# Two-layer transformer kernel: layer 2's q/k columns in lane-major order, and its q/k tiles loaded in 12 transfers per batch instead of 36

## The chip, the cores and the metric

The kernel runs on one core of a Trainium2 chip (trn2). The metric is the device time of one execution in microseconds (us). Smaller is better. Times shown as runs are whole executions; the profile is one further execution, read by its trace.

## The reference, cut to what matters

The input is 16 batches of 512 tokens with 128 features. Four layers follow one another, each added to its input: a linear attention, a mixture of 8 experts, a softmax attention, and a mixture of 16 experts that choose their tokens. The change is in the softmax attention, called layer 2 here (`L1_attn` in the code):

```python
q = jnp.einsum('btc,oc->bto', x, Wq).reshape(B, T, H, D)      # H = 16 heads, D = 8
k = jnp.einsum('btc,oc->bto', x, Wk).reshape(B, T, H, D)
v = jnp.einsum('btc,oc->bto', x, Wv).reshape(B, T, H, D)
att = jnp.einsum('bqhd,bkhd->bhqk', q, k) * SCALE
att = jnp.where(band_mask, -inf, att)
att = softmax(att, axis=-1)
out = jnp.einsum('bhqk,bkhd->bqhd', att, v)
```

## The kernel before, in words

**Stages.** The work of the first three layers is pipelined over the batches. `looped` runs, for each batch, an x phase and a y phase on every engine; 13 of the passes are a hardware loop (`Fori(1, BATCH - 2)`, line L277), the first and last ones are written out. In one pass the x phase holds the expert layer of batch i+1 (L669, L677, L685, L695 on TensorE), the row maxima of the attention of batch i, and the end of batch i-1. The y phase holds the attention scores and outputs of batch i, the linear attention of batch i+2, and the q, k, v of batch i+1. After the loop come the choice of tokens (L1420 to L1561) and the 16 experts, which the change doesn't touch. Each engine has its own instruction list, written out by hand; they meet at semaphores only.

**q and k in three parts.** Layer 2's q and k are computed as 128 features x 512 tokens in `facc` (`r_q` L706, `r_k` L710, with `w_q1` and `w_k1`). ScalarE, VectorE and GpSimd split them into three bf16 parts each, whose sum is the fp32 value, in `qkp` (L1029, L1368, L486, L488). SyncE stores `qkp` to `qk_parts` in HBM, q and k apart (`part_dmas`, L313), waits for both, and loads it back in another layout (`back_dmas`, L317 to L331).

**QT and KT.** These two tiles hold, for each head and token, 72 rows: all 9 pairs of a q part i and a k part j, with 8 lanes each. The scores of a head are then one matmul over 72 (or 75) rows. In `back_dmas` a feature of `qk_parts` is (head, lane), the lane being the inner index; a transfer takes part i of q, or part j of k, to 8 partitions, one per lane, and 8 heads of 512 tokens in each:

```python
for i in range(PARTS):
    for j in range(PARTS):
        r = (i * PARTS + j) * HD
        for t, w, part in ((QT, 0, i), (KT, 1, j)):
            sp.dma_start(t[r:r + HD, heads], qk_parts[b, w, part].rearrange("(h d) t -> d h t", d=HD)[:, heads])
```

So half 0 (heads 0 to 7) and half 1 (heads 8 to 15) take 18 transfers each. Half 0 may start when the scores of the first 20 fills of the y phase are done, half 1 when all 40 are (`s_st`, last written by L582).

**Who waits for them.** The x phase on TensorE begins with `fill(0)`: scores L585 (with the mask L587) into one of three banks `ba`, from fill 0 on with half 0 and from fill 20 on with half 1. VectorE reduces each bank to row maxima (L1263 to L1268), and TensorE may write a bank again only then. SyncE's own order in a pass is: `load_x` (xin, L359), `residual_dmas` (L352), `max_dmas` (QT from nmT, L339), `row_dmas` (L345), `part_dmas` (L313), `back_dmas` half 0, half 1 (L330). VectorE needs xin at L1135 in the x phase.

Of the kernel before, what the change touches and what calls it, by code (L numbers as in the profile page):

```python
# [14 lines left out]
F32, BF16, F16, I32, I16 = mybir.dt.float32, mybir.dt.bfloat16, mybir.dt.float16, mybir.dt.int32, mybir.dt.int16  # L15
# [4 lines left out]
P = 128  # L20
BATCH, SEQ, D = 16, 512, 128
# [3 lines left out]
HEADS, HD = 16, 8  # L25
# [10 lines left out]
PARTS = 3  # L36
# [8 lines left out]
def build_kernel(nc, a, out):  # L45
    ctx = ExitStack()
    with ctx:
# [5 lines left out]
        def sb1(name, shape, dt=F32):  # L53

            return early.enter_context(nc.sbuf_tensor(name, shape, dt))
# [2 lines left out]
            return ctx.enter_context(nc.semaphore(name))  # L58


        qk_parts = nc.dram_tensor("qk_parts", (BATCH, 2, PARTS, P, SEQ), BF16, kind="Internal").ap()
        xn_rows = nc.dram_tensor("xn_rows", (TOK, ROW), F32, kind="Internal").ap()
        out_rows = out.rearrange("b s d -> (b s) d")
        lists = nc.dram_tensor("lists", (E1, CAP), I32, kind="Internal").ap()
# [3 lines left out]
        facc = ctx.enter_context(nc.psum_tensor("facc", [P, 512], F32))  # L68
# [33 lines left out]
        w_q1 = sb1("w_q1", [P, D])  # L102
        w_k1 = sb1("w_k1", [P, D])
        w_v1 = sb1("w_v1", [P, D])
        w_o1 = sb1("w_o1", [P, D])
        router_w = sb1("router_w", [P, E1])
        router_b = sb1("router_b", [P, E1])
# [41 lines left out]
        b_nT = sb1("b_nT", [P, SEQ])  # L149
        qkp = sb1("qkp", [P, 2, PARTS, SEQ], BF16)  # L150
        qkr = sb1("qkr", [P, 2, SEQ])
        vp = sb1("vp", [P, Q, HEADS, 32])
        QT = sb1("QT", [P, HEADS, SEQ], BF16)
        KT = sb1("KT", [P, HEADS, SEQ], BF16)
# [31 lines left out]
        def sb3(name, shape, dt=F32):  # L186
# [54 lines left out]
        names = """s_wfront s_wexperts s_wback s_cst s_one s_scal s_x s_lnf s_xres s_varf s_rsf s_T1 s_nT1 s_kvq s_kvqe s_sq  # L241
            s_kqn s_kvt s_kvm s_qT s_qnT s_kvo s_kvoc s_at0 s_x1 s_x1n s_T2 s_nT2 s_lgm s_lge s_exf s_lgx s_gp s_gTp s_gT
            s_h1 s_h3 s_gb s_gbc s_sil s_t s_h s_hs s_ym s_yT s_yTt s_x2 s_fc
            s_pad s_lnb s_varb s_rsb s_T3 s_nT3 s_q s_k s_v s_p1 s_r1 s_p2 s_p3 s_vp s_qkw s_qk0 s_qk1 s_S s_red s_nmp s_nmt
            s_nmT s_mx0 s_mx1 s_st s_exp s_pv s_oT s_tr s_norm s_aTt s_aT s_wo s_x3 s_row s_T4 s_nT4 s_l1 s_l1c
            s_g1x s_g1e s_rowd s_mstep s_x3d s_gn s_gnd
            s_vart s_rst s_rstep s_tc s_rden s_LTt s_cnt s_tot s_sr s_gtc s_gtt s_eqt s_rc s_slT s_slot s_ramp s_hot s_hot_t s_list s_keys s_cand s_cnt3 s_set s_gth s_gthc s_low s_diag s_gatec s_gj s_found s_idx s_bc1 s_ldw s_ldr
# [1 line left out]
        S = {n: sem(n) for n in names}  # L249
# [40 lines left out]
        def _(sp):  # L290
# [17 lines left out]
            def part_dmas(b):  # L308

                for w in range(2):  # L310
                    sp.wait_ge(S["s_p3"], 2 * b + w + 1)
                    apart(sp)
                    sp.dma_start(qk_parts[b, w].rearrange("c p t -> p c t"), qkp[:, w]).then_inc(S["s_qkw"], 16)  # L313
                sp.wait_ge(S["s_qkw"], 32 * b + 32)
                apart(sp)

            def back_dmas(b, half):  # L317

                if isinstance(b, int) and b == 0:
                    sp.wait_ge(S["s_pad"], 3)  # L320
                else:

                    sp.wait_ge(S["s_st"], FILLS * b - (1 - half) * FILLS // 2)
                    apart(sp)
                heads = slice(half * HEADS // 2, (half + 1) * HEADS // 2)
                for i in range(PARTS):
                    for j in range(PARTS):
                        r = (i * PARTS + j) * HD
                        for t, w, part in ((QT, 0, i), (KT, 1, j)):
                            sp.dma_start(t[r:r + HD, heads], qk_parts[b, w, part].rearrange("(h d) t -> d h t", d=HD)[:, heads])\  # L330
                              .then_inc(S[f"s_qk{half}"], 16)  # L331

            def max_dmas(b, half):

# [267 lines left out]
        def _(pe):  # L602
# [95 lines left out]
            def r_turn(r):  # L698
                if isinstance(r, int) and r == 0:
                    pe.wait_ge(S["s_wback"], BW)  # L700
                pe.wait_ge(S["s_lnb"], r + 1)
                transposes(facc, b_n, "s_T3")

            def r_q(r):
                pe.wait_ge(S["s_nT3"], r + 1)
                pe.matmul(facc[:], lhsT=w_q1[:], rhs=b_nT[:], start=True, stop=True).then_inc(S["s_q"], 1)  # L706

            def r_k(r):
                pe.wait_ge(S["s_r1"], 2 * r + 1)
                pe.matmul(facc[:], lhsT=w_k1[:], rhs=b_nT[:], start=True, stop=True).then_inc(S["s_k"], 1)  # L710

            def r_v(r):
                pe.wait_ge(S["s_r1"], 2 * r + 2)
# [41 lines left out]
            def x_phase(f, b, t, g):  # L755
                def fill(n):
                    if b is None:
                        return
                    if n == 0:
                        pe.wait_ge(S["s_qk0"], 16 * 2 * PARTS * PARTS * (b + 1))  # L760
                        pe.wait_ge(S["s_exp"], FILLS * b)
                    if n == FILLS // 2:
                        pe.wait_ge(S["s_qk1"], 16 * 2 * PARTS * PARTS * (b + 1))
                    if n >= 3:
                        pe.wait_ge(S["s_red"], FILLS * b + n - 2)
                    scores(pe, b, n, False)
# [201 lines left out]
        def _(act):  # L968
# [37 lines left out]
            def y_phase(b, f, r, t):  # L1006
# [18 lines left out]
                                   ACT.Square).then_inc(S["s_sq"], 1)  # L1025
                exps(1)
                if r is not None:
                    act.wait_ge(S["s_qkw"], 32 * r)
                    copy(qkp[:, 0, 0], facc[:], "s_q", r + 1, "s_p1")  # L1029
                exps(2)  # L1030
                if r is not None:
# [59 lines left out]
        def _(dve):  # L1091
# [261 lines left out]
            def r_norm(r):  # L1353
                rc.start(r)
                if isinstance(r, int) and r == 0:
                    dve.wait_ge(S["s_wback"], BW)
                dve.wait_ge(S["s_x2"], r + 1)
                apart(dve)
                stats(rc, x3_of(r), b_st, b_mv)
                dve.tensor_scalar(b_ve[:], b_mv[:, :, 1], EPS, None, ALU.add).then_inc(S["s_varb"], 1)  # L1360
# [270 lines left out]
```

## Time and profile before

| what | value |
|---|---|
| median of 3 runs | 2110.64 us (2103.11 to 2110.79) |
| the profiled execution's own time | 2108.77 us |
| its span, first to last instruction | 2107.0 us |
| mean granted TensorE clock | 0.883 of 2.4 GHz |
| TensorE, VectorE, ScalarE, GpSimd busy | 77%, 59%, 37%, 24% of the span |
| DMA: bytes, packets | 86.56 MB, 113452 |
| HBM read, written | 58.95 MB, 25.72 MB |

In the profile PE is TensorE's matmuls and PEld its weight loads, DVE is VectorE, ACT ScalarE, POOL GpSimd and SP SyncE; a q behind a name (SPq, DVEq) is that engine's sequencer, which issues DMAs and branches. Busy time says how much an engine did, the waits and the chain of waits say what it stood for. "Issue" is time in which an engine waited for nothing that the profile records. Stretches are in microseconds from the start of the span.

### The profile page before, as it was taken

How to read it: one execution, taken by the hardware profiler on the slowest of the kernel's cores; microseconds unless marked ns; L12 is line 12 of the kernel's file. 1: busy time of each engine (PE TensorE's matmuls, PEld its weight loads, DVE VectorE, ACT ScalarE, POOL GpSimd, SP SyncE). 2: the span in 40 equal slices, each digit the busy share in tenths (PEclk: the TensorE clock that was granted, in tenths of full speed). 3: DMA queues.
4: the chain of work that ended last, by engine and by line, in shares of the span. 5: the costliest groups of instructions: out<-in, count | busy, mean ns of one | idle time of the engine just before them, and what ended most of it. 6: DMA issues, size and time to landing. Idle time of an engine off the chain costs nothing.

```text
span 2107.0 us, 34513 instructions
## 1 busy us (share of the span) xinstructions
PE 1619.2 (77%) x10136; PEld 907.4 (43%) x10136; DVE 1236.6 (59%) x3717; ACT 778.5 (37%) x1387; POOL 501.6 (24%) x487
## 2 busy tenths in 40 slices
PE   3869898979787878888888888798889781137765
PEld 2335454535353434444444444444454441135554
DVE  5456767666667575757575757575766526861111
ACT  1225252525252525252525252525254242134331
POOL 2311212121212121212121212121212002006887
PEclk7879999989899989899989899999999875568897
DMA  2041321313131313130313130404031400024444
GB/s 63 16 50 33 40 50 27 50 26 51 25 52 25 52 24 57 19 59 18 58 18 59 17 61 15 64 12 63 13 58 20 65 7 10 0 39 86 89 89 59
DMA packets 113452, 86.56 MB, mean 41 GB/s; under 512 B 21569, under 2 KB 107841, under 8 KB 113345
## 3 DMA queue, kind: packets, MB, share of 16 engines
q1 hardware_dynamic: 102080, 76.58, 21.4%
q0 software_dynamic: 11264, 8.92, 3.2%
q14 instruction: 86, 0.70, 0.2%
q8 instruction: 22, 0.36, 0.1%
HBM read 58.95 MB, written 25.72 MB: 40 GB/s over the span
## 4 chain that ended last, share of the span: by engine, by line
PE 47%; DVE 17%; issue 17%; POOL 5%; DMA 4%; ACT 4%; SPq 2%; DVEq 1%; ACTq 0%; POOLq 0%
PE ba L580 6%; PE bo L839 5%; PE facc L695 5%; PE fa L669 5%; PE ba L585 5%; PE fa L685 5%; POOL out L552 3%; SPq L330 2%; ACT probs L1015 2%; DVE passed L1460 2%; DVE nm L1263 2%; PE ba L587 2%; PE ba L582 2%; POOL got L522 2%; DMA KT<-qk_parts 1%
## 5 line engine op out<-in xcount | busy, mean ns | idle before, releaser
L585 PE MATMUL ba<-KT,QT 72*128 72x512 bf16 (+3 forms) x1024 | 262.2, 320 | 182.5 <-DVE nm L1263 129.2
L1015 ACT ACTIVATE probs<-ba 128x512 f32<-128x512 f32 x640 | 330.5, 640 | 97.7 <-PE ba L582 96.9
L459 POOL TENSOR_TENSOR hh<-th,gb 128x512 f32<-128x512 f32 x128 | 161.9, 1265 | 697.5 <-ACT gb L971 427.0
L580 PE MATMUL ba<-QT,KT 75*128 75x512 bf16 (+3 forms) x1024 | 253.3, 310 | 35.2 <-ACT probs L1015 28.7
L1263 DVE TENSOR_REDUCE nm<-ba 128x1 f32<-128x512 f32 x256 | 174.6, 682 | 179.5 <-issue 131.2
L585 PEld LDWEIGHTS ba<-KT,QT 72*128 72x128 bf16 x1024 | 105.0, 103 | 344.5 <-DVE nm L1263 155.8
L587 PE MATMUL ba<-mask_q,identb 128*128 128x128 bf16 x1024 | 200.8, 230 | 0.0
L987 ACT ACTIVATE sil<-fa 128x512 f32<-128x512 f32 x160 | 95.4, 596 | 274.9 <-PE fa L669 274.8
L582 PE MATMUL ba<-mask_k,identb 128*128 128x128 bf16 x1024 | 195.5, 224 | 0.0
L669 PE MATMUL fa<-f_nT,w 128*128 128x512 f32 x320 | 187.1, 669 | 1.2 <-ACT sc L1046 1.2
L685 PE MATMUL fa<-f_nT,w 128*128 128x512 f32 x320 | 181.1, 649 | 0.0
L971 ACT ACTIVATE gb<-fa 128x512 f32<-128x512 f32 x128 | 76.5, 598 | 278.7 <-PE fa L677 245.4
L580 PEld LDWEIGHTS ba<-QT,KT 75*128 75x128 bf16 x1024 | 101.7, 99 | 156.5 <-ACT probs L1015 104.7
L695 PE MATMUL facc<-hh,w 128*128 128x512 f32 x320 | 166.2, 602 | 0.0
L839 PE MATMUL bo<-probs,vp 128*32 128x512 f32 (+3 forms) x2048 | 155.2, 444 | 0.8 <-DVE ao L1384 0.8
L1265 DVE TENSOR_REDUCE nm<-ba 128x1 f32<-128x384 f32 x256 | 140.6, 549 | 25.1 <-PE ba L587 25.0
L587 PEld LDWEIGHTS ba<-mask_q,identb 128*128 128x128 bf16 x1024 | 106.3, 104 | 81.7 <-issue 79.5
L452 POOL TENSOR_TENSOR b_rs<-b_ve,mhalf 128x4 f32<-128x4 f32 x48 | 48.5, 1010 | 336.4 <-DVE b_ve L1360 229.1
L1375 DVE COPY oT<-bo 128x512 f32<-128x512 f32 x64 | 44.1, 690 | 116.4 <-PE bo L839 115.4
L552 POOL DMA_INDIRECT out<-contrib,cur x64 | 100.7, 1573 | 30.5 <-issue 18.6
L839 PEld LDWEIGHTS bo<-probs,vp 128*32 128x32 f32 x2048 | 60.8, 111 | 99.2 <-issue 69.9
L582 PEld LDWEIGHTS ba<-mask_k,identb 128*128 128x128 bf16 x1024 | 102.6, 100 | 1.6 <-issue 0.7
(284 smaller groups left out, 2643.2 us busy)
## 6 DMA issues: line engine op xcount, KB each, us to landing
QT<-qk_parts SPq DMA_DIRECT2D x288, 64.0 KB
KT<-qk_parts SPq DMA_DIRECT2D x288, 64.0 KB
qk_parts<-qkp SPq DMA_DIRECT2D x32, 384.0 KB, 2.5
fc<-in_L_ffn_fc_weight SPq DMA_DIRECT2D x32, 256.0 KB
xin<-in_L_attn_x SPq DMA_DIRECT2D x16, 256.0 KB, 13.4
out<-x SPq DMA_DIRECT2D x16, 256.0 KB, 2.3
xn_rows<-row SPq DMA_DIRECT2D x16, 256.0 KB, 2.4
w<-in_L_w SPq DMA_DIRECT2D x3, 640.0 KB, 6.7
```

The source lines that it names most:

```text
L459: pool.tensor_tensor(hh[:, e % 2], th[:, e % 2], gb[:, e % 2], ALU.mult).then_inc(S["s_h"], 1)
L552: pool.indirect_dma_start(out_rows, bass.IndirectOffsetOnAxis(cur[k][:, c:c + 1], 0), contrib[k % 2][:, c], None, compute_op=ALU.add).then ...
L580: pe.matmul(bank[:, col:col + w], lhsT=KT[0:K_ROWS, head, blk * P:(blk + 1) * P], rhs=QT[0:K_ROWS, head, blk * P:], start=True, stop=False)
L582: last = pe.matmul(bank[:, col:col + P], lhsT=identb[:], rhs=mask_k[:], start=False, stop=True)
L585: pe.matmul(bank[:, col:col + w], lhsT=QT[0:QK_ROWS, head, blk * P:(blk + 1) * P], rhs=KT[0:QK_ROWS, head, 0:w], start=True, stop=False)
L587: last = pe.matmul(bank[:, col + w - P:col + w], lhsT=identb[:], rhs=mask_q[:], start=False, stop=True)
L669: pe.matmul(fa[0][:], lhsT=w1[:, e], rhs=f_nT[:], start=True, stop=True).then_inc(S["s_h1"], 1)
L685: pe.matmul(fa[1][:], lhsT=w3[:, e], rhs=f_nT[:], start=True, stop=True).then_inc(S["s_h3"], 1)
L695: pe.matmul(facc[:], lhsT=w2[:, e], rhs=hh[:, e % 2], start=e == 0, stop=e == U0 - 1).then_inc(S["s_ym"], 1)
L839: last = pe.matmul(bo[32 * j:32 * j + 32, blk * P:], lhsT=vp[:, blk, 4 * k + j], rhs=prob_block(4 * k + j, blk), start=blk == 0, stop=blk ...
L1015: act.activation(probs[:, pair % 3, f_], ba[n % 3][:], ACT.Exp, scale=SCALE).then_inc(S["s_exp"], 1)
L1263: last = dve.tensor_reduce(nm[:, 3, h:h + 1], bank[:], X, ALU.max, negate=True)
```

## The change

Layer 2's q and k features are ordered (lane, head) instead of (head, lane). A new tile `w_qk` holds both weights with their columns reordered; VectorE makes it once, by two copies in front of batch 0's `r_norm`, and TensorE waits for them once. `qk_parts` has five places per batch for q and for k. All three parts of each are stored to the first three, and a third store puts k's parts 0 and 1 into places 3 and 4. The 9 pairs are now (part p of q, part (shift + p) mod 3 of k), so that each of three shifts takes three neighbouring places at once: 24 partitions of QT or KT, with 8 heads x 512 tokens that lie together in HBM (8 KB). Half 0 and half 1 take 6 transfers each. SyncE's wait before the loads counts three stores.

```diff
-        qk_parts = nc.dram_tensor("qk_parts", (BATCH, 2, PARTS, P, SEQ), BF16, kind="Internal").ap()
+        qk_parts = nc.dram_tensor("qk_parts", (BATCH, 2, 2 * PARTS - 1, P, SEQ), BF16, kind="Internal").ap()
...
+        w_qk = sb1("w_qk", [P, 2, HD, HEADS])
...
                 for w in range(2):
                     sp.wait_ge(S["s_p3"], 2 * b + w + 1)
                     apart(sp)
-                    sp.dma_start(qk_parts[b, w].rearrange("c p t -> p c t"), qkp[:, w]).then_inc(S["s_qkw"], 16)
-                sp.wait_ge(S["s_qkw"], 32 * b + 32)
+                    sp.dma_start(qk_parts[b, w].rearrange("c p t -> p c t")[:, 0:PARTS], qkp[:, w]).then_inc(S["s_qkw"], 16)
+                sp.dma_start(qk_parts[b, 1].rearrange("c p t -> p c t")[:, PARTS:], qkp[:, 1, 0:PARTS - 1]).then_inc(S["s_qkw"], 16)
+                sp.wait_ge(S["s_qkw"], 48 * b + 48)
                 apart(sp)
...
-                for i in range(PARTS):
-                    for j in range(PARTS):
-                        r = (i * PARTS + j) * HD
-                        for t, w, part in ((QT, 0, i), (KT, 1, j)):
-                            sp.dma_start(t[r:r + HD, heads], qk_parts[b, w, part].rearrange("(h d) t -> d h t", d=HD)[:, heads])\
-                              .then_inc(S[f"s_qk{half}"], 16)
+                for shift in range(PARTS):
+                    r = slice(shift * PARTS * HD, (shift + 1) * PARTS * HD)
+                    for t, w, part in ((QT, 0, 0), (KT, 1, shift)):
+                        rows = qk_parts[b, w, part:part + PARTS].rearrange("c (d h) t -> (c d) h t", h=HEADS)
+                        sp.dma_start(t[r, heads], rows[:, heads]).then_inc(S[f"s_qk{half}"], 16)
...
                 if isinstance(r, int) and r == 0:
                     pe.wait_ge(S["s_wback"], BW)
+                    pe.wait_ge(S["s_wqk"], 2)
...
-                pe.matmul(facc[:], lhsT=w_q1[:], rhs=b_nT[:], start=True, stop=True).then_inc(S["s_q"], 1)
+                pe.matmul(facc[:], lhsT=w_qk[:, 0].rearrange("p d h -> p (d h)"), rhs=b_nT[:], start=True, stop=True).then_inc(S["s_q"], 1)
...
-                pe.matmul(facc[:], lhsT=w_k1[:], rhs=b_nT[:], start=True, stop=True).then_inc(S["s_k"], 1)
+                pe.matmul(facc[:], lhsT=w_qk[:, 1].rearrange("p d h -> p (d h)"), rhs=b_nT[:], start=True, stop=True).then_inc(S["s_k"], 1)
...
-                        pe.wait_ge(S["s_qk0"], 16 * 2 * PARTS * PARTS * (b + 1))
+                        pe.wait_ge(S["s_qk0"], 16 * 2 * PARTS * (b + 1))
...
-                        pe.wait_ge(S["s_qk1"], 16 * 2 * PARTS * PARTS * (b + 1))
+                        pe.wait_ge(S["s_qk1"], 16 * 2 * PARTS * (b + 1))
...
-                    act.wait_ge(S["s_qkw"], 32 * r)
+                    act.wait_ge(S["s_qkw"], 48 * r)
...
                 if isinstance(r, int) and r == 0:
                     dve.wait_ge(S["s_wback"], BW)
+                    for w, t in enumerate((w_q1, w_k1)):
+                        dve.tensor_copy(w_qk[:, w], t[:].rearrange("p (h d) -> p d h", d=HD)).then_inc(S["s_wqk"], 1)
```

SyncE, in the loop body: the end of the stores and the start of half 0, before. ISA stands for register and semaphore work, and a DMA's shape is partitions x elements.

```order
L313 DMA qk_parts<-qkp 128x3x512
L314 ISA
L323 ISA [waits s_qkw]
L330 DMA QT<-qk_parts 8x8x512 [waits s_st]
L330 DMA KT<-qk_parts 8x8x512
L330 DMA QT<-qk_parts 8x8x512
```

The same place now:

```order
L314 DMA qk_parts<-qkp 128x3x512
L315 ISA
L315 DMA qk_parts<-qkp 128x2x512
L316 ISA
L325 ISA [waits s_qkw]
L332 DMA QT<-qk_parts 24x4096 [waits s_st]
L332 DMA KT<-qk_parts 24x4096
L332 DMA QT<-qk_parts 24x4096
```

A third store stands ahead of the wait for the stores, and each load is 24 x 4096 elements in one run where it was 8 x 8 x 512; the loop body has 12 of them where it had 36.

VectorE, at the written-out start of batch 0's part in layer 2, now (x<-facc is the residual sum that the expert layer ends with):

```order
L1353 TENSOR_TENSOR x<-facc,x 128x512 [waits s_yTt]
L1360 COPY w_qk<-w_q 128x128 [waits s_wback]
L1360 COPY w_qk<-w_k 128x128
L1137 BN_STATS b_st<-x 128x6 [waits s_x2]
```

The two copies stand between the residual sum and the statistics; before, the statistics followed at once, and they took the wait for the weights (`s_wback`) with them.

## Rows read from the trace of the kernel before

**Rows 1.** The page: busy us of each engine (share of the span) and instructions

```profile
PE 1619.2 (77%) x10136; PEld 907.4 (43%) x10136; DVE 1236.6 (59%) x3717; ACT 778.5 (37%) x1387; POOL 501.6 (24%) x487
```

**Rows 2.** The table of waits: engine, line <- releaser: us in total, times, longest

```profile
DVE nm L1263 <- issue: 131.2, 12, 12.4
PE ba L585 <- DVE nm L1263: 129.2, 17, 11.8
```

**Rows 3.** The chain of waits, 1020 to 1065 us: start, us, what

```profile
1047.39 0.06 DVEq L277
1047.45 11.83 issue
```

**Rows 4.** Loop line L277, 1040 to 1065, then VectorE's, whole span: ns min/median/max, starts

```profile
L277 PEldq COMPARE_BRANCH  x1: 207/207/207, 1044.4 to 1044.4; - x1
L277 PEldq FUSED_REGOPS  x1: 50/50/50, 1044.7 to 1044.7; - x1
...
L277 DVEq COMPARE_BRANCH  x13: 55/63/63, 319.5 to 1572.0; - x13
```

**Rows 5.** The timeline of SyncE's queue, 1024 to 1050 us: start, us, what

```profile
1024.63 0.32 SPq L330 DMA_DIRECT2D QT<-qk_parts  x1
...
1039.24 0.28 SPq L330 DMA_DIRECT2D QT<-qk_parts  x1
...
1049.50 0.40 SPq L359 DMA_DIRECT2D xin<-in_L_attn_x  x1
```

**Rows 6.** Stretches of one pass: us, busy us of each engine, PEclk, DMA share, GB/s

```profile
1036.00:1047.40 11.40, 8.18 (x76) 5.12 (x74) 7.10 (x36) 3.87 (x8) 0.00 (x0) 1.00 0.59 64
1047.40:1059.30 11.90, 2.02 (x13) 0.93 (x11) 0.20 (x1) 2.36 (x3) 0.00 (x0) 0.67 0.65 80
1059.30:1065.00 5.70, 4.86 (x14) 2.41 (x15) 4.33 (x9) 1.08 (x2) 0.94 (x1) 0.50 0.31 47
```

**Rows 7.** DMA issues: count, KB each, median us to landing

```profile
QT<-qk_parts SPq DMA_DIRECT2D x288, 64.0 KB
...
qk_parts<-qkp SPq DMA_DIRECT2D x32, 384.0 KB, 2.5
...
xin<-in_L_attn_x SPq DMA_DIRECT2D x16, 256.0 KB, 13.4
out<-x SPq DMA_DIRECT2D x16, 256.0 KB, 2.3
```

**Rows 8.** Stretches of other transfers: the first weights, and a store of qk_parts

```profile
11.00:14.00 3.00, 0.00 (x0) 0.00 (x0) 2.42 (x11) 0.21 (x1) 0.51 (x1) 1.00 1.02 418
1022.00:1024.00 2.00, 2.00 (x20) 1.68 (x18) 0.29 (x1) 1.36 (x3) 0.00 (x0) 1.00 0.58 197
```

**Rows 9.** First pass of the loop, its branch stall (chain), and half 0's first load

```profile
220.50:319.50 99.00, 89.19 (x572) 47.21 (x571) 68.38 (x210) 42.16 (x77) 19.90 (x18) 0.97 0.28 46
...
295.18 0.33 SPq L330 DMA_DIRECT2D QT<-qk_parts  x1
...
319.60 7.66 issue
```

**Rows 10.** First pass: xin's wait, TensorE behind it, the clock; and a 128x128 operation

```profile
236.60 0.87 DVE L1135 BATCH_NORM_STATS2 f_st<-xin 128x6 f32<-128x128 f32 x4 [5.25 <-DMA xin<-in_L_attn_x]
...
238.98 0.39 PE L585 MATMUL ba<-KT,QT 72*128 72x256 bf16 x1 [4.20 <-DVE nm L1266]
...
236.00:242.00 6.00, 3.02 (x9) 1.32 (x10) 5.19 (x18) 0.00 (x0) 1.48 (x2) 0.75 0.00 0
...
1039.77 0.29 DVE L1384 TENSOR_TENSOR ao<-bo,rden 128x128 f32<-128x128 f32 x1
```

**Rows 11.** Batch 0 and the last batch: TensorE's waits for KT

```profile
125.45 0.61 PE L585 MATMUL ba<-KT,QT 72*128 72x512 bf16 x1 [10.73 <-DMA KT<-qk_parts]
...
1661.03 0.61 PE L585 MATMUL ba<-KT,QT 72*128 72x512 bf16 x1 [4.88 <-DMA KT<-qk_parts]
...
1678.62 0.61 PE L585 MATMUL ba<-KT,QT 72*128 72x512 bf16 x1 [4.29 <-DMA KT<-qk_parts]
```

More of the change, by code:

```diff
@@ L243, in build_kernel @@
             s_h1 s_h3 s_gb s_gbc s_sil s_t s_h s_hs s_ym s_yT s_yTt s_x2 s_fc
-            s_pad s_lnb s_varb s_rsb s_T3 s_nT3 s_q s_k s_v s_p1 s_r1 s_p2 s_p3 s_vp s_qkw s_qk0 s_qk1 s_S s_red s_nmp s_nmt
+            s_pad s_wqk s_lnb s_varb s_rsb s_T3 s_nT3 s_q s_k s_v s_p1 s_r1 s_p2 s_p3 s_vp s_qkw s_qk0 s_qk1 s_S s_red s_nmp s_nmt
             s_nmT s_mx0 s_mx1 s_st s_exp s_pv s_oT s_tr s_norm s_aTt s_aT s_wo s_x3 s_row s_T4 s_nT4 s_l1 s_l1c
```

## The prediction

> **What bounds the kernel now.** I read the page first [rows 1]: TensorE is busy 77% of the span and VectorE 59%, so neither fills it. The table of waits comes next [rows 2]. Among VectorE's waits one is released by nothing that the profile shows: "issue", 131.2 us in 12 times, always before the first maxima reduction (L1263). TensorE's longest wait, 129.2 us in 17 times, is on that same reduction. The chain of waits [rows 3] gives the place: VectorE's branch at the end of the loop body (DVEq L277) at 1047.39, then 11.83 us of nothing, then the first instruction of the next pass. The records of the loop's own line [rows 4] show that TensorE has no such stall: its branch is at 1044.4 and its counter for the next pass at 1044.7. VectorE branches 13 times, 319.5 to 1572.0 us, so a pass is 104.4 us; 12 branches are taken, 12 stalls follow, 10.9 us each.
>
> Why so long? SyncE's queue [rows 5] shows the load of QT and KT: half 0 is issued from 1024.63, half 1 from 1039.24, and xin only behind it at 1049.50. Meanwhile the DMA traffic is flat at 64 GB/s [rows 6]. Both halves are 36 transfers of 64 KB [rows 7], 2.36 MB, 37 us at 64 GB/s: from 1024.6 to about 1062. A store of 128 partitions of the same 1 KB runs reaches 197 GB/s, and the weights at the start 418 GB/s [rows 8], so the loads' shape is slow, not the memory. What is issued behind them is late too: xin, 256 KB, lands after 13.4 us at the median, an equal store after 2.3 [rows 7]. The stall fits: VectorE resumes 34.8 us after the first load of half 0 in this pass. In the first stalled pass half 0 is issued at 295.18, 24.3 us ahead of the branch where it is 22.8 here, and the stall there is 7.66 us, ending 32 us after the first load [rows 9]. So the end of the stall follows the backlog of the loads, not the branch. I read it as VectorE fetching the loop's first instructions through DMA engines that are choked by the loads. The Trainium skill ("Runtime: NRT & Kernel Launch", Instruction fetch mechanics) says that a taken branch out of a small window forces such a fetch; the trace agrees, in that the stall follows the taken branch on VectorE.
>
> **The change part by part.**
>
> *Loads.* Per batch 36 transfers of 8 partitions x 8 runs of 1 KB become 12 of 24 partitions, one 8 KB run each; bytes stay 2.36 MB. Their rate is not in the trace, so I bound it. From below: 64 GB/s as now, 18.4 us a half. From above: the 418 GB/s of the weights, 2.8 us. Between them I scale 64 GB/s by the partitions written at once, 8 to 24: a factor of 3, 192 GB/s, 6.1 us a half. I take this, since it is nearest to the store at 197 GB/s in the same pass [rows 8]. If half of the factor comes, 1.5, it is 96 GB/s and 12.3 us: the slow case. A factor of 1.5 is also what a rule of the skill gives ("DMA: Bandwidth & Descriptors", Why a DMA increments its semaphore by 16 and not by 1): the engines used are the largest number up to 16 that divides the outer size, 8 for 8 and 12 for 24. The skill's "SBUF — State Buffer" (Door 1) instead counts ports, four neighbouring partitions to one: 2 before, 6 now, a factor of 3. By the first rule alone the time would be that of the slow case below, 2037 us, by the second that of the forecast.
>
> *SyncE.* 36 issues become 12. Half 1 still starts at 1039.24, when TensorE's last use of the tiles frees it, and with 6 issues in place of 18 is out some 2 us later instead of 10; xin goes out there, not at 1049.5.
>
> *The third store* (256 KB, issued behind the second, before the loads): 0.4 us to issue and 1.3 us at 197 GB/s, 1.6 us later for half 0. In the loop this is covered: half 0 would land at 1024.6 + 1.6 + 6.1 + 2 = 1034.3, and TensorE branches into the next pass at 1044.4 [rows 4]. Without that cover it costs 1.6 us, as in batch 0.
>
> *The two reordering copies* on VectorE happen once; a 128x128 piece takes 0.29 us [rows 10]: 0.6 us. The matmuls keep their shape (L706, L710), so 0.
>
> *The branch stall.* Half 1 has left the queues by 1039.2 + 6.1 = 1045.3, ahead of VectorE's branch at 1047.4. What is left is the fetch itself. Below it is bounded by TensorE's 0.3 us [rows 4], above by the backlog at 96 GB/s: half 1 ends at 1051.5, 4.1 us after the branch, plus the fetch, 6.6. For an unhindered fetch I take 2.5 us, what a store of qk_parts needs to land [rows 7]. The stall falls from 10.9 to 2.5: 8.4 us a pass.
>
> *The clock behind it.* In the stall TensorE's granted clock falls to 0.50 (1.2 GHz) for the 5.7 us after it [rows 6]: 4.9 us busy at half speed, 2.4 us lost. TensorE's gap becomes some 2.5 us in place of about 11. In the first pass it idled 4.20 us, and the six microseconds around show 0.75, half of them at full clock [rows 10]; with a gap shorter than that I count the clock as kept. The bound below is 0.
>
> *A check on the sum.* The first pass in the loop has no branch before it, and is 99.0 us long [rows 9]. In it VectorE waits 5.25 us for xin, itself behind the loads, and the clock is at half for half of 6 us, 3.0 of it, and 1.5 lost [rows 10]. Without both: 92.2 us. A pass with the 2.5 us fetch is then 94.7, against 104.4: 9.7 us. The terms above give 10.8; I take 9.7, since it is a whole pass as it ran. What is late next inside the pass is again TensorE with the maxima, as now.
>
> *Outside the stalls.* First pass: 5.25 + 1.5 = 6.8. Batch 0: TensorE waits 10.73 us for KT [rows 11]; half 0 took 1.18 MB / 64 GB/s = 18.4 us and takes 6.1 + 1.6 for the third store: 10.7 less, of which I count 10 (by the slow bound 18.4 - 13.9 = 4.5). Last batch: two waits for KT, 4.88 and 4.29: 9.2 us.
>
> **Sum:** 12 x 9.7 + 6.8 + 10 + 9.2 - 0.6 = 142 us off the profiled execution's 2108.8 (span 2107.0), 1967 us. The median of the runs is 2110.6, 0.1% more; a difference of 0.5% (10.5 us) is about what a measurement here can tell from none.
>
> **The rivals.**
>
> *The loads gain only half.* 12.3 us a half: the stall is 6.6, the clock falls as before. 12 x 4.3 + 6.8 + 4.5 + 9.2 = 72 us: 2037. For it: the store at 197 GB/s works on all 128 partitions, the loads on 24. Against it: the same loads on 8 have 64 already. Chance 0.14.
>
> *The fetch has a price of its own.* Some 11 us per taken branch whatever the queues hold; the gain is 6.8 + 10 + 9.2 = 26 us: 2083. For it: the mean of 10.9 and the longest of 12.4 us [rows 2] lie close together, as a constant would. Against it: the one of 7.66 us, and xin, late by the same amount. The skill's rule stands on this rival's side ("DMA: Bandwidth & Descriptors", Queues, rings and completion order): an engine takes turns between its rows packet by packet, so a fetch should not stand behind a whole backlog. Chance 0.10.
>
> *The loads are the same.* The transfer may be cut up again below the program, and end at 64 GB/s; then only issues are saved, and the time stays within a few us of 2109. Against it: SyncE's list has one 24 x 4096 transfer in place of three. Chance 0.04.
>
> *Slower: long runs into few partitions move at less than before.* Backlog ends at half 0's issue plus 2.36 MB over the rate, and half 0 is now 1.6 us later, so it decides below 2.36 MB / 35.4 us = 67 GB/s. At 50 GB/s it ends at 1073.4 instead of 1062: 12 more per pass, 12 x 12 + 12 in the first pass + some 10 in the first and last batch: 2275. For it: an 8 KB run goes into one partition, and no row has such a run. Against it: the weights' runs, 5 KB to a partition, at 418 GB/s [rows 8]. Chance 0.04.
>
> **How the numbers follow.** Forecast: 0.68, 1967 us, its own range 1925 (a fetch of 0.3 us: 2.2 less in 12 passes, and the 1.1 between the two sums, 40 us) to 1990 (a fetch of 4.5 us: 24 more). The slow-load case reaches 2037, so I close the range at 1925 to 2042; outside are the three rivals at 2083 and above, together 0.18. Faster by over 0.5%: 0.68 + 0.14 + 0.10 = 0.92; within: 0.04; slower: 0.04.
>
> **What would show each step.** VectorE's "issue" wait before L1263 near 30 us in 12 times, not 131; behind its branch the loop counter 2 to 4 us later; the slices behind the issue of a half near 190 GB/s and empty after 6 us; xin landing in 3 to 5 us; the granted clock near 1.00 through the start of a pass; TensorE's waits for KT gone; a pass of 94 to 95 us. Wrong would be: the loads short and the stall still near 11 (the third case), or slices behind the issue under 100 GB/s (the second).

## The result and the profile after

| | kernel before | changed kernel |
|---|---|---|
| median of 4 runs each, one chip | 2106.88 us (2095.60 to 2110.79) | 1978.94 us (1976.47 to 1981.08) |
| ratio, 95% interval | | 0.9401, 0.9359 to 0.9442 |
| the profiled execution | 2108.77 us, span 2107.0 | 1980.44 us, span 1978.7 |
| mean granted TensorE clock | 0.883 | 0.907 |

The change takes 6.0% off. 1967 us was forecast, within 1925 to 2042: the time is 12 us above the point and inside the range. One run in this document, e2's of 2054.1 us, lies over 1.5% above the fastest of its kernel (2022.8 us); e2's median and ratio leave it out.

The page of the changed kernel, its busy times, against [rows 1]:

```profile
PE 1604.5 (81%) x10090; PEld 903.9 (46%) x10136; DVE 1237.3 (63%) x3719; ACT 778.6 (39%) x1387; POOL 501.7 (25%) x487
```

VectorE does what it did, in a span that is 128.3 us shorter: what went was waiting, not work. TensorE's busy time is down by 15 us; how much of that is the clock and how much the 46 matmul records fewer (10090 for 10136, some 7 us at their mean of 0.16 us) is not told apart here. The tables of waits, against [rows 2]:

```profile
DVE nm L1265 <- issue: 38.3, 12, 3.7
...
PE ba L586 <- DVE nm L1265: 43.5, 22, 3.9
```

The stalls are still 12, one for each taken branch, but 38.3 us together and not 131.2. TensorE's wait on the same reduction went with them, from 129.2 to 43.5. The chain of waits, 865 to 885 us, against [rows 3], and the loop line (now L278) over the whole span, against [rows 4]:

```profile
872.38 0.06 DVEq L278
872.45 3.44 issue
875.88 0.06 DVEq L278
...
876.00 0.70 DVE nm L1265
```

```profile
L278 DVEq COMPARE_BRANCH  x13: 55/63/63, 296.6 to 1452.5; - x13
```

A pass is (1452.5 - 296.6) / 12 = 96.3 us, where it was 104.4. The twelve stalls of the chain lie between 2.83 and 3.75 us, 3.2 in the mean. SyncE's queue over 820 to 880 us, against [rows 5]:

```profile
841.59 5.65 SPq L314 DMA_DIRECT2D qk_parts<-qkp  x2
847.42 0.37 SPq L315 DMA_DIRECT2D qk_parts<-qkp  x1
850.41 0.36 SPq L332 DMA_DIRECT2D QT<-qk_parts  x1
...
852.68 0.30 SPq L332 DMA_DIRECT2D KT<-qk_parts  x1
864.21 0.30 SPq L332 DMA_DIRECT2D QT<-qk_parts  x1
...
866.48 0.30 SPq L332 DMA_DIRECT2D KT<-qk_parts  x1
867.37 0.40 SPq L360 DMA_DIRECT2D xin<-in_L_attn_x  x1
```

Each half is out in 2.6 us, and xin is issued 5.0 us ahead of VectorE's branch at 872.38 instead of 2.1 behind it. What the engines move meanwhile (columns as in [rows 6]):

```profile
850.40:856.50 6.10, 6.06 (x66) 3.70 (x58) 2.08 (x6) 3.40 (x9) 0.00 (x0) 1.00 0.65 146
864.20:870.40 6.20, 5.38 (x58) 3.58 (x56) 5.12 (x25) 1.52 (x4) 0.00 (x0) 1.00 0.73 153
870.40:872.40 2.00, 2.00 (x9) 0.79 (x9) 1.84 (x12) 1.04 (x1) 0.00 (x0) 1.00 0.71 148
872.40:876.00 3.60, 0.71 (x7) 0.26 (x5) 0.19 (x2) 1.32 (x3) 0.00 (x0) 0.98 0.31 57
876.00:880.00 4.00, 3.04 (x9) 1.53 (x11) 3.21 (x7) 0.16 (x1) 0.00 (x0) 0.50 0.01 2
```

150 GB/s where 64 stood before, 8 us a half, and then xin: the traffic still reaches a little past the branch (57 GB/s over the stall). The last row is what the forecast did not count: TensorE's granted clock is still at 0.50 (1.2 GHz) behind the stall. The landings, against [rows 7]:

```profile
QT<-qk_parts SPq DMA_DIRECT2D x96, 192.0 KB
...
xin<-in_L_attn_x SPq DMA_DIRECT2D x16, 256.0 KB, 7.1
qk_parts<-qkp SPq DMA_DIRECT2D x16, 256.0 KB, 2.7
```

xin lands after 7.1 us, before 13.4. No wait for xin or for KT stands in the tables any more; those of [rows 10] and [rows 11] are gone. The first pass of the loop, without a branch ahead of it, and the two behind it, against [rows 9]:

```profile
205.40:296.60 91.20, 85.46 (x569) 45.86 (x571) 68.42 (x210) 41.88 (x77) 19.91 (x18) 1.00 0.19 46
296.60:391.20 94.60, 85.38 (x569) 45.88 (x571) 68.49 (x210) 41.80 (x77) 19.89 (x18) 1.00 0.19 45
391.20:488.90 97.70, 87.85 (x569) 46.83 (x570) 68.54 (x210) 41.74 (x77) 19.89 (x18) 0.97 0.18 44
```

**Where the 128 us come from.** Branches and spans cut the two profiles into the same pieces:

| piece | before | after | gain | forecast |
|---|---|---|---|---|
| start to the loop | 220.5 | 205.4 | 15.1 | 10 - 0.6 |
| first pass | 99.0 | 91.2 | 7.8 | 6.8 |
| 12 passes with a stall | 1252.5 | 1155.9 | 96.6 | 116.4 |
| last branch to the end | 535.0 | 526.2 | 8.8 | 9.2 |
| span | 2107.0 | 1978.7 | 128.3 | 141.8 |

So all of the shortfall lies in the twelve passes, 8.1 us each and not 9.7, and 5.7 us came back ahead of the loop.

**The fetch itself is in the profile.** The prediction called the stall "released by nothing that the profile shows". The view of the DMA queues does show it: beside SyncE's queue there is one of the kind "instruction", with packets of 8 KB. Narrow windows around the stalls find exactly one such packet inside each: in all 12 of before, all 12 of the changed kernel, the same in the runs e4 to e8 told below, and in the nine stalls of e3 that the chain of waits shows. One pass of each (us):

| kernel | branch | the packet moves | VectorE goes on |
|---|---|---|---|
| before | 1047.4 | 1056.7 | 1059.3 |
| e6 (8 partitions, 8 KB runs) | 914.0 | 921.0 | 923.0 |
| changed kernel | 872.4 | 873.9 | 875.9 |
| e7 (queues nearly empty) | 870.2 | 871.2 | 873.0 |

With nearly empty queues the packet moves about 1 us after the branch and VectorE goes on 1.8 us later. Over all stalls the second part stays between 1.7 and 2.9 us; it is the first part that grows, to between 7.7 and 9.9 us in eleven stalls of before (5.4 in its first). And it grows by what is queued ahead: in before the packet moves when SyncE's queue has moved 2.16 to 2.30 MB of the 2.29 to 2.36 MB that it had been given by the time of the branch (2.59 of 2.62 in the first stall, where xin was issued ahead of the branch). It does not wait for the 0.32 to 0.46 MB that are then left in eleven of the stalls, xin, issued behind the branch, among them: in the pass shown they move until about 1062.5, 3 us after VectorE went on.

### The profile page after: what moved, and what is told of

The parts are those of the page before. It is cut to its first block, busy times and chain, and to the rows that moved or that the text cites. A ratio compares the mean times of both kernels' runs of the same rounds, so it can differ in the third digit from the quotient of the medians.

```text
span 1978.7 us, 33763 instructions
## 1 busy us (share of the span) xinstructions
PE 1604.5 (81%) x10090; PEld 903.9 (46%) x10136; DVE 1237.3 (63%) x3719; ACT 778.6 (39%) x1387; POOL 501.7 (25%) x487
## 4 chain that ended last, share of the span: by engine, by line
PE 50%; DVE 19%; issue 12%; POOL 5%; ACT 4%; DMA 2%; DVEq 1%; SPq 0%; ACTq 0%; POOLq 0%
PE ba L581 6%; PE bo L841 6%; PE ba L586 5%; PE facc L696 5%; PE fa L686 5%; PE fa L670 5%; POOL out L553 3%; ACT probs L1017 2%; DVE nm L1265 2%; PE ba L583 2%; DVE passed L1464 2%; PE ba L588 2%; POOL got L523 2%; PE ba L957 1%; PE bo L848 1%
## 5 line engine op out<-in xcount | busy, mean ns | idle before, releaser
L1017 ACT ACTIVATE probs<-ba 128x512 f32<-128x512 f32 x640 | 330.3, 636 | 97.3 <-PE ba L583 96.5
L586 PE MATMUL ba<-KT,QT 72*128 72x512 bf16 (+3 forms) x1024 | 256.3, 313 | 68.2 <-DVE nm L1265 43.5
L1265 DVE TENSOR_REDUCE nm<-ba 128x1 f32<-128x512 f32 x256 | 174.8, 683 | 70.0 <-issue 38.3
L588 PE MATMUL ba<-mask_q,identb 128*128 128x128 bf16 x1024 | 196.8, 226 | 0.0
L670 PE MATMUL fa<-f_nT,w 128*128 128x512 f32 x320 | 183.8, 658 | 1.2 <-ACT sc L1048 1.2
L686 PE MATMUL fa<-f_nT,w 128*128 128x512 f32 x320 | 177.5, 637 | 0.1
L1572 DVE TENSOR_TENSOR ysum<-ba,fb 128x512 f32<-128x512 f32 x16 | 11.1, 692 | 158.5 <-PE ba L957 158.5
```

The source lines that it names most:

```text
L586: pe.matmul(bank[:, col:col + w], lhsT=QT[0:QK_ROWS, head, blk * P:(blk + 1) * P], rhs=KT[0:QK_ROWS, head, 0:w], start=True, stop=False)
L588: last = pe.matmul(bank[:, col + w - P:col + w], lhsT=identb[:], rhs=mask_q[:], start=False, stop=True)
L670: pe.matmul(fa[0][:], lhsT=w1[:, e], rhs=f_nT[:], start=True, stop=True).then_inc(S["s_h1"], 1)
L686: pe.matmul(fa[1][:], lhsT=w3[:, e], rhs=f_nT[:], start=True, stop=True).then_inc(S["s_h3"], 1)
L1017: act.activation(probs[:, pair % 3, f_], ba[n % 3][:], ACT.Exp, scale=SCALE).then_inc(S["s_exp"], 1)
L1265: last = dve.tensor_reduce(nm[:, 3, h:h + 1], bank[:], X, ALU.max, negate=True)
```

## The experiments

Theory A is that of the forecast: a taken branch makes VectorE fetch the loop's first instructions, the fetch waits behind the loads of QT and KT, and so the stall ends when the loads issued ahead of the branch are through. Rivals: the stall belongs to the work at the top of the pass; the gain comes from the loads' own waits; run length or the number of transfers matters, not the partitions. All nine were run on the changed kernel unless "before" is said.

| run | edit | us | ratio to before, 95% | stalls, mean us | pass |
|---|---|---|---|---|---|
| before | | 2106.9 | | 10.9 | 104.4 |
| changed kernel | | 1978.9 | 0.940 (0.936 to 0.944) | 3.2 | 96.3 |
| e1 | VectorE's loop written out | 1919.1 | 0.907 (0.903 to 0.912) | none | 91.1 |
| e2 | before, VectorE's loop written out | 2028.4, three runs | 0.960 (0.953 to 0.967) | none | |
| e3 | before, no loads of half 1 | 1984.9, one run | | 2.8 | 95.2 |
| e5 | no loads of half 1 | 1970.1, one run | | 2.7 | 95.7 |
| e4 | 24 partitions, 1 KB runs | 1998.2 | 0.943 (0.939 to 0.947) | 3.9 | 97.7 |
| e6 | 8 partitions, 8 KB runs | 2062.8 | 0.977 (0.973 to 0.981) | 8.9 | 102.5 |
| e8 | no third store | 1980.0 | 0.937 (0.934 to 0.940) | 3.2 | 96.6 |
| e9 | TensorE kept busy at the branch | 1970.4 | 0.930 (0.926 to 0.934) | 2.7 | 95.6 |
| e7 | xin issued earlier | 1970.2 | 0.930 (0.927 to 0.933) | 2.7 | 95.5 |

The ratios are against runs of before on the same chip (medians 2115.2 for e1 to e4, 2115.8 for e5, e6, e8 and e9, 2116.6 for e7). The last two columns are of the profiled execution; a pass is the distance of VectorE's first to last branch, divided by 12 (for e1 that of SyncE's stores of `row`). On the chip of the first comparison before took 2106.9 us, on these 9 us more. So a difference of up to some 9 us between 1978.9 and a whole time of this table can be the chip's, and by the ratios it can come out otherwise; the stalls and passes of the profiles are the firmer measure there.

**e1 and e2: no branch on VectorE.** The other engines keep their loops.

```diff
+            if unrolled:
+                for i in range(1, BATCH - 2):
+                    x_phase(i + 1, i, i - 1, i + 2)
+                    y_phase(i, i + 2, i + 1, i - 1)
...
-            looped(dve, x_phase, y_phase)
+            looped(dve, x_phase, y_phase, unrolled=True)
```

> The changed kernel with VectorE's list alone written out for all 13 passes, so that it takes no branch. Theory A (the stall at the start of a pass is an instruction fetch that a taken branch forces): VectorE's issue wait before the first maxima, 38.3 us in 12 times, goes to under 3 us, a pass takes 91 us as the first one does (205.4 to 296.6) in place of 96.3, and the time falls by about 60 us to 1919. Rival B (the stall belongs to the start of the x phase, whatever the branch): the wait stays near 3.2 us in each pass, 1979. Rival C (a list of some 8000 instructions that is streamed once falls behind): the issue waits spread over other lines, 1960 or more.

> The kernel before with the same edit and its 36 short loads. Theory A: the 131.2 us of issue wait are gone although the backlog is as long as before; every pass is then like the first, 99.0 us instead of 104.4, since VectorE still waits some 5 us for xin behind the loads: about 2044. If xin is late in the first pass only, 1962. Rival B: stall and time stay, 2107. Rival C (a backlog of 37 us also delays the fetches of a straight list, past what is fetched ahead): issue waits of several us at other lines of VectorE, 2070 or more.

e1 hit its number. SyncE's stores of `row`, once a batch, show the pass, in the changed kernel first and then in e1:

```profile
831.41 0.43 SPq L346 DMA_DIRECT2D xn_rows<-row  x1
928.94 0.41 SPq L346 DMA_DIRECT2D xn_rows<-row  x1
1025.48 0.41 SPq L346 DMA_DIRECT2D xn_rows<-row  x1
```

```profile
898.27 0.41 SPq L351 DMA_DIRECT2D xn_rows<-row  x1
988.77 0.41 SPq L351 DMA_DIRECT2D xn_rows<-row  x1
```

97.5 and 96.5 us become 90.5; over the loop e1's lie between 90.5 and 92.4. 12 x (96.3 - 91.2) = 61 us were to be had, and 1978.9 - 1919.1 = 60 came (69 by the ratios). The stall is the branch's, and so is the loss of clock behind it. e1 beats both kernels. e2 separates the two costs of the slow loads in before. Its branch stalls are gone too, and what is left are waits on the loads themselves:

```profile
DVE f_st L1140 <- DMA xin<-in_L_attn_x: 77.0, 14, 8.3
```

```profile
PE ba L590 <- DMA KT<-qk_parts: 33.0, 14, 10.5
```

77 us for xin (landing after 16.0 us at the median, 13.4 in before) are nearly all new: before has 8.4 us in two waits, for in the loop the stall covered them. TensorE's wait for KT was 26.4 us in 13 times and is 33.0 in 14. So slow loads cost time without the fetch as well. 2028.4 us lie 16 us below the 2044 of theory A, and far from those of its rivals. Of the 196 us between before (2115.2) and e1, writing out the loop alone gives 85 (71 to 99, by the interval of the ratio), the loads alone 128; so some 17 us are in both. (The profile is of the run of 2054.1 us, so only its waits are read.)

**e3 and e5: less behind the branch.** Both leave out the loads of half 1 after batch 0; TensorE's wait for half 1 then asks for batch 0's only.

```diff
+                if half == 1 and not (isinstance(b, int) and b == 0):
+                    return
```

> The kernel before without the loads of half 1 after batch 0: heads 8 to 15 of later batches are computed with batch 0's q and k. SyncE's waits stay, the branch stays. Theory A with the backlog: half 0's 1.18 MB at 64 GB/s are through by 1043, before VectorE's branch at 1047.4, so the stall falls from 10.9 to about 3 us, as in the changed kernel, and the time to some 1980 to 2000. Rival (the price of the fetch depends on the kernel's shape of transfers or on the number of issues, not on what is queued at the branch): the stall stays over 8 us and the time over 2060.

> The changed kernel without the loads of half 1 after batch 0 (heads 8 to 15 of later batches use batch 0's q and k). In the changed kernel half 1 is issued 8.2 us before VectorE's branch and needs about 8 us at 150 GB/s. Theory (a part of the 3.2 us stall is still the end of that backlog; the kernel before with half 1 left out had 2.7): the stall falls to 2.7, the time by 6 to 12 us. Rival (3.2 us is the fetch alone): stall and time stay within 0.1 and 3 us.

In before, with the loads of half 0 still 8 partitions wide, the stall falls from 10.9 to between 2.69 and 3.05 us (e3, the nine stalls that its tables put to "issue"), although nothing in front of the branch or behind it changed on VectorE. That rules out a fixed price near 11 us. It takes away 18 issues as well as their bytes; that the bytes count is read from the packets above and from e6. In the changed kernel the same edit takes off only 0.5 us of stall (3.2 to 2.7) and 0.6 a pass, 12 x 0.6 = 7 us; the one run is 9 us shorter. The two ends meet at 2.7 us, the fetch with the queues empty. The rows of waits, of e3 and of e5:

```profile
DVE nm L1265 <- issue: 24.8, 9, 3.0
```

```profile
DVE nm L1267 <- issue: 32.6, 12, 3.0
```

**e4 and e6: which part of the new shape counts.** The change makes two things at once: 24 partitions for 8, and 8 KB runs for 1 KB. e4 keeps the first (heads of the two halves lie alternately in HBM, so that a half's runs are 1 KB), e6 the second (each load is cut into three of 8 partitions).

```diff
-                        rows = qk_parts[b, w, part:part + PARTS].rearrange("c (d h) t -> (c d) h t", h=HEADS)
-                        sp.dma_start(t[r, heads], rows[:, heads])
+                        rows = qk_parts[b, w, part:part + PARTS].rearrange("c (d h x) t -> (c d) h x t", h=HEADS // 2, x=2)
+                        sp.dma_start(t[r, heads], rows[:, :, half])
```

```diff
+                        for p in range(PARTS):
+                            r = (shift * PARTS + p) * HD
+                            rows = qk_parts[b, w, part + p].rearrange("(d h) t -> d h t", h=HEADS)
+                            sp.dma_start(t[r:r + HD, heads], rows[:, heads])
```

> The changed kernel with runs of 1 KB: the halves' heads are interleaved in the column order, so each of the 12 transfers still goes to 24 partitions, but reads 8 runs of 1 KB for each. Theory (the rate follows the partitions a transfer spreads over): the slices behind an issue stay near 150 GB/s as in the changed kernel (146 and 153), the stall stays at 3.2 to 4 us, 1979 to 1985. Rival (the length of the runs made the loads fast): the rate falls to 64 to 96 GB/s, the stall to 6 us or more, 2030 to 2100.

> The changed kernel with each load cut into three of 8 partitions: 8 KB runs as now, 36 transfers per batch as before. Theory (the rate follows the partitions a transfer spreads over): 60 to 75 GB/s behind an issue, a stall of 9 to 12 us, and a time near the kernel before, 2080 to 2110. Rival (the long runs matter): over 100 GB/s and a stall under 6 us, 2030 or less.

Stretches behind the issue of half 0 and of half 1, first of e4, then of e6:

```profile
863.90:869.50 5.60, 5.60 (x64) 3.54 (x62) 1.20 (x4) 2.90 (x8) 0.00 (x0) 1.00 0.50 117
878.20:884.00 5.80, 4.99 (x56) 3.29 (x54) 4.73 (x23) 1.51 (x4) 0.00 (x0) 1.00 0.53 122
```

```profile
892.00:899.00 7.00, 6.91 (x71) 4.02 (x64) 2.85 (x10) 4.30 (x11) 0.00 (x0) 1.00 0.45 83
...
905.80:914.00 8.20, 7.39 (x65) 4.36 (x64) 6.92 (x35) 2.53 (x5) 0.00 (x0) 1.00 0.50 88
914.00:920.00 6.00, 0.78 (x7) 0.31 (x5) 0.23 (x1) 1.39 (x3) 0.00 (x0) 0.91 0.61 106
```

| | 1 KB runs | 8 KB runs |
|---|---|---|
| 8 partitions | 64 GB/s (before) | 83 to 88 GB/s (e6) |
| 24 partitions | 117 to 122 GB/s (e4) | 146 to 153 GB/s (changed) |

The partitions give a factor of 1.7 to 1.9 in either column, the run length one of 1.25 to 1.4 in either row, together 2.3 to 2.4. The DMA engines' mean busy share is 0.59 in before ([rows 6]), 0.45 to 0.50 in e6, 0.50 to 0.53 in e4 and 0.65 to 0.73 in the changed kernel; what it is in the number of partitions that makes the rate, no run tells apart. By e6 8 KB runs alone would have given 53 us, by e4 24 partitions alone 117 us. Both outcomes lie outside what was expected of them: e4 was put at no more than 1985 and is 1998, e6 at no less than 2080 and is 2063. Run length weighs more than theory A had it. In e4 part of it is the issue, for each of its transfers has 192 runs of 1 KB where the changed kernel's has 24 of 8 KB:

```profile
881.89 0.78 SPq L332 DMA_DIRECT2D QT<-qk_parts  x1
882.86 0.78 SPq L332 DMA_DIRECT2D KT<-qk_parts  x1
```

0.78 us for each and not 0.30 (before's transfers, of 64 runs, took 0.28): a half takes 5.5 us to issue instead of 2.6. At 120 GB/s it needs 9.8 us to move, so the issue is not all of it.

The backlog rule holds in e6. The chain of waits, 905 to 930 us:

```profile
914.02 0.06 DVEq L278
914.09 8.87 issue
```

Half 0 was issued at 892.03. 2.36 MB at 85 GB/s are 27.8 us, to 919.8; the fetch's packet moves at 921.0 and the stall ends at 923.0. xin (issued at 914.35, behind the branch) is in the queues too. The changed kernel's stall has 3.2 us with loads that end about at the branch, e4's 3.9 with loads that end a little later, e6's 8.9 and before's 10.9 with loads that end well behind it: the same order throughout.

**e8: the third store.** KT takes its parts from the same three places for every shift.

```diff
-                sp.dma_start(qk_parts[b, 1].rearrange("c p t -> p c t")[:, PARTS:], qkp[:, 1, 0:PARTS - 1]).then_inc(S["s_qkw"], 16)
-                sp.wait_ge(S["s_qkw"], 48 * b + 48)
+                sp.wait_ge(S["s_qkw"], 32 * b + 32)
...
-                    for t, w, part in ((QT, 0, 0), (KT, 1, shift)):
+                    for t, w, part in ((QT, 0, 0), (KT, 1, 0)):
```

> The changed kernel without the third store; KT's loads take places 0 to 2 for every shift, so that k's parts are paired wrongly and six of the nine products stand twice or not at all. Theory (the third store is covered everywhere but in batch 0): half 0 is issued 1 to 1.6 us sooner, TensorE does not notice, time equal to the changed kernel's within 4 us. Rival (256 KB more to HBM per batch hold up what follows them): 10 us less or more.

1980.01 against 1978.94 us, stalls of 3.2 us in both, a pass of 96.6 against 96.3: 4.2 MB of stores more cost nothing that can be told from the chips' difference. In the pass at 844 us half 0 is issued 8.1 us after the stores begin, where the changed kernel takes 8.8: 0.8 us sooner and not 1 to 1.6.

**e9: the clock.** In the loop's passes TensorE does 14 matmuls into a bank that nobody reads, as soon as VectorE's last work ahead of the branch is done.

```diff
+                if t is not None and not isinstance(t, int):
+                    pe.wait_ge(S["s_norm"], 4 * t + 4)
+                    for _ in range(14):
+                        pe.matmul(bo[:], lhsT=identb[:], rhs=pick[:, 0:4].rearrange("p e c -> p (e c)"), start=True, stop=True)
```

> The changed kernel with 14 matmuls of 128x512 bf16 on TensorE in each pass of the loop, some 3 us at full clock, between the gates' transposes and fill 3, into a bank that is overwritten before it is read: work that nobody needs, in the gap that VectorE's stall leaves. Theory (the 1.9 us per pass beyond stall and straight pass are TensorE at half clock after its gap): the granted clock stays at 1.00 over the start of a pass, a pass takes 94.4 to 95.0 us in place of 96.3, 1957 to 1965. Rival (those 1.9 us are something else, the clock costs nothing here): 1977 or more.

The clock at the top of the pass is kept, as meant. What that is worth stays unclear: by the medians 8.6 us come of it, of the 14 to 22 expected, by the ratios 21, and e9's four runs lie between 1958.5 and 1977.4 us. The profile is of the longest of them. Stretches of it from one pass: ahead of the branch, and across the stall.

```profile
865.00:874.00 9.00, 8.18 (x58) 4.48 (x59) 6.48 (x33) 1.73 (x4) 0.00 (x0) 0.81 0.79 160
874.00:878.00 4.00, 3.84 (x21) 1.76 (x21) 1.29 (x4) 1.56 (x3) 0.00 (x0) 1.00 0.02 5
```

In this run the loss has moved. Ahead of the branch, where the changed kernel has 1.00, the clock now stands at 0.81 over 9 us: 1.7 us lost there, in place of 1.9 behind the branch. 91.2 + 2.7 + 1.7 = 95.6, which is the pass of e9. The kernel before has the same once, ahead of its first branch and without any filler: 0.83 over the 9.8 us from 309.8 to 319.6. Why the clock falls there, with TensorE busy for 8.2 of 9 us, no run here tells. The gain that is left in this run is the shorter stall (2.7 for 3.2): the queues are empty by then (5 GB/s in the second row).

**e7: xin ahead of the stores.** One question was left: does xin, issued just before the branch, hold up the fetch? (SyncE's last pass is written out for it.)

```diff
-            with sp.Fori(1, BATCH - 2) as i:
-                load_x(i + 2)
+            load_x(3)
+
+            def one_pass(i, last=False):
...
+                if not last:
+                    load_x(i + 3)
                 part_dmas(i + 1)
```

> The changed kernel, with SyncE issuing xin one batch earlier and ahead of the stores of qk_parts in its pass, so that nothing but the loads of half 1 stands in the DMA queues at VectorE's branch; nothing is left out. Theory (the 3.2 us stall is a fetch of 2.7 us plus about 0.5 us behind the end of the loads and xin): xin's 256 KB no longer share the engines with the fetch, the stall falls by at most 0.5 us, the issue wait in front of the maxima stays between 32 and 39 us in 12 times, the clock at a pass's start stays near 0.8, and the time is 1970 to 1981 us. Rival (xin, issued at the branch, is what lengthens the fetch and the rest of the fetch is small): the stall falls to 1.5 us or less and the clock is kept: 1940 us or less.

1970.2 us is the lower end of what theory A said, and 12 x (96.3 - 95.5) = 10 us come from the passes of the profiles, so this gain is not the chip's. xin lands in 2.9 us, and the stall is at its floor. The chain of waits, 868 to 876 us, and the stretches across and behind the stall:

```profile
870.18 0.06 DVEq L278
870.25 2.70 issue
```

```profile
870.20:873.00 2.80, 0.71 (x7) 0.27 (x5) 0.19 (x1) 1.32 (x3) 0.00 (x0) 1.00 0.02 3
873.00:876.00 3.00, 2.19 (x6) 1.03 (x7) 2.94 (x7) 0.00 (x0) 0.00 (x0) 0.65 0.01 3
876.00:880.00 4.00, 3.78 (x18) 2.07 (x18) 2.32 (x7) 1.68 (x3) 1.26 (x1) 0.84 0.00 0
```

3 GB/s during the stall, and it still takes 2.70 us: that is the fetch with nothing ahead of it. The clock behind it gives away 3.0 x 0.35 + 4.0 x 0.16 = 1.7 us even so. Of the edits tried, only taking the branch away removed both (e1).

## Why the prediction was right, and which steps left it 12 us low

**What bounds the kernel: right.** The stall at VectorE's taken branch was the bound, and its length was the loads issued ahead of it: the fetch's packet moves when they are through, e3 empties the queues behind half 0 and the stall falls to its floor without any change to the loads' shape, and e1 takes the branch away and the whole cost goes. Where the prediction has the whole backlog, up to 1062, as what the stall ends with, it is only the part ahead of the branch: the packet moves at 1056.7. "The fetch has a price of its own" (0.10) falls as a price of 11 us; as a price of 2.7 it is true. The 2.5 that the forecast took was borrowed from the landing of a store, a transfer of another kind, so that it lies this near is in part luck. The Trainium skill ("Runtime: NRT & Kernel Launch", Instruction fetch mechanics) says that a taken branch to a target outside a small window forces a fetch. The trace agrees: each stall holds one packet of the instruction queue, and without the branch (e1) there is no stall. The Trainium skill's rule that a DMA engine takes turns between its rows packet by packet ("DMA: Bandwidth & Descriptors", Queues, rings and completion order) would, as the prediction read it, have the fetch pass the backlog. The trace differs: the fetch's packet, in a queue of its own, moves 9.2 us after the branch, with 2.18 of the 2.29 MB ahead of it through. (That xin is late behind the loads says nothing on this rule, since both are in SyncE's queue.)

**Loads, a factor of 3 and 192 GB/s: the size was off.** They reach 146 to 153 GB/s, a factor of 2.3 to 2.4, and a half takes 8 us. It lies between the two factors that the forecast weighed, 1.5 and 3. By e4 and e6 neither describes it: partitions give 1.7 to 1.9 of it and run length, for which the forecast had counted nothing, 1.25 to 1.4. For the time this mattered little: half 1 now ends at the branch instead of 2 us ahead of it. That the miss cost so little is in part luck: at half the factor the forecast itself had a stall of 6.6 us.

**The branch stall, 10.9 to 2.5: off by 0.7.** Measured 3.2: 2.7 of fetch (e5, e7, e9) and 0.5 because the last of the loads and xin, issued ahead of the branch, are still moving. 12 x 0.7 = 8 us.

**The clock "counted as kept": wrong, and the largest miss.** TensorE waits up to 3.9 us for the first reduction now, and in eleven of the twelve passes the clock falls behind it, after the shortest stall (2.83 us) too; only the first pass with a stall, of 3.32 us, keeps it (94.6 us, where the next takes 97.7). The pass of 96.3 less 91.2 and 3.2 leaves 1.9 us, 12 x 1.9 = 23 us. The forecast leaned on one row, the 4.20 us of [rows 10] with half of the following six microseconds at full clock, and read "half kept" as "kept when the gap is shorter". The stalls of 2.7 us in e7 (clock 0.65 behind the one shown) show that it is not. The passes without a stall were 1 us shorter than the forecast had them (91.2 against 92.2): the first pass of before had also lost 1.7 us of clock ahead of its branch (0.83 over 9.8 us), which the forecast's 1.5 did not hold. So the "whole pass as it ran" of 94.7 took the miss back in part, by chance: 0.7 + 1.9 - 1.0 = 1.6 a pass, which is the 20 us of the table within rounding.

**Outside the stalls: 6 us better.** TensorE's waits for KT are gone as said. Ahead of the loop 15.1 us came where 9.4 stood: TensorE's waits for KT were 10.9 us and all went, and the forecast had overlooked a wait for xin in batch 0. The chain of waits of before, 120 to 221 us, shows it once it is asked for:

```profile
128.30 14.73 DMA xin<-in_L_attn_x
```

xin is issued at 128.30 behind the backlog, and VectorE stands 3.2 us for it. In the changed kernel it is issued at 109.23. The last 1 us of the 15.1 is not traced. **Third store, copies, matmuls at next to nothing: not contradicted** (e8 for the store; the others were not run alone, and the pieces of the table show no loss that would need them).

**The other rivals.** "Only half" (2037) was at 96 GB/s with a stall of 6.6: e6, at 83 to 88 GB/s, is about that case and has 2063. "The loads are the same" and "long runs are slower" are refuted by the rates; at 8 partitions, too, long runs are the faster ones (83 to 88 GB/s against 64).

## What to carry to other kernels

When an engine stands still at a loop's branch for "issue", look for a packet of the instruction queue inside the stall and at what the DMA queues hold ahead of it, and price the stall as the fetch with empty queues (here 2.7 us) plus what is left of the loads issued before the branch, plus the clock that TensorE loses behind it. Of the two ways to make such a load faster, more partitions gave more here than longer runs. What is urgent and small is better issued ahead of it (e7). It can pay to write out the loop of the engine that stalls and leave those of the others: here that was worth 60 us on top of a change that gave 128.

## What the hardware showed that was not expected

- A taken branch of VectorE fetches one 8 KB packet through the DMA engines. In the kernel before it moved only when 2.16 to 2.30 MB of the 2.29 to 2.36 MB that SyncE's queue had been given ahead of the branch were through, and it passed what was given behind it, xin for one.
- A DMA into 8 partitions stays at 64 GB/s with 1 KB runs and at 83 to 88 GB/s with 8 KB runs; into 24 partitions it has 117 to 122 and 146 to 153. From 8 to 24 partitions the rate grows by 1.7 to 1.9, from 1 KB to 8 KB runs by 1.25 to 1.4.
- Issuing a load of 24 partitions takes 0.30 us with one run of 8 KB to each partition and 0.78 us with eight of 1 KB; one of 8 partitions with eight of 1 KB takes 0.28 us.
- A stall of 2.7 us, with TensorE working for 0.7 us of it, can be enough for its granted clock to stand at 0.65 in the 3 us behind (e7, the pass at 870 us; after the loop's first stall, of 2.9 us, it stayed at 1.00). Filling that gap with matmuls moved the loss to the end of the pass in the profiled run (e9); why stays unexplained.
